# Two layer normalisations moved from VectorE to ScalarE in a three-stage kernel

## The reference

```
x = _layernorm(x + L0_attn(x))     # a state-space layer, 64 heads   -> x1
x = _layernorm(x + L0_ffn(x))      # gated, 704 wide, integer weights -> x2
x = _layernorm(x + L1_attn(x))     # running sums, gated 1024 wide    -> x3
x = _layernorm(x + L1_ffn(x))      # 16 experts, 4 a token            -> out

def _layernorm(x, eps=1e-05):
    return (x - mean(x)) / sqrt(var(x) + eps)
```

## Time and profile before

| what | value |
|---|---|
| median of 3 runs | 2046.97 us (2040.39 to 2054.52) |
| span of the profiled execution, first to last instruction | 2052.9 us |
| that execution's own time | not listed apart from the runs; its span is within their range |
| TensorE matmuls busy | 1773.4 us, 86% |
| TensorE weight loads busy | 1227.3 us, 60% |
| VectorE busy | 1322.3 us, 64% |
| ScalarE busy | 730.2 us, 36% |
| GpSimd busy | 857.8 us, 42% |
| mean granted TensorE clock | 0.948 of full speed |

### The profile page before, as it was taken

The page is one execution under the profiler, slowest core; times in us unless marked ns, Lnnn a source line. Parts: engine busy times, 40 slices in busy tenths (PEclk is TensorE's granted clock), DMA queues, the critical chain, the costliest instruction groups (busy, mean ns, idle before and its releaser), DMA issues. The chain is left out here.

```text
span 2052.9 us, 34902 instructions
## 1 busy us (share of the span) xinstructions
PE 1773.4 (86%) x8724; PEld 1227.3 (60%) x8725; DVE 1322.3 (64%) x2876; ACT 730.2 (36%) x1384; POOL 857.8 (42%) x856
## 2 busy tenths in 40 slices
PE   3589999989999999999998998873899999999980
PEld 2257667667576576676765765652455566666650
DVE  4678878878787888787788787622344444444435
ACT  3244344344343443443444434221222233233223
POOL 2033243333432432433324323223466676666654
PEclk8799999999999999999999999986899999999995
DMA  5423132231231321322313313283999999999997
GB/s 204 141 93 108 28 113 71 69 107 55 82 105 33 111 81 53 107 62 82 107 37 97 103 31 103 71 252 97 195 174 164 171 181 175 173 178 177 176 144 250
DMA packets 385800, 244.37 MB, mean 119 GB/s; under 512 B 269072, under 2 KB 364624, under 8 KB 385360
## 3 DMA queue, kind: packets, MB, share of 16 engines
q1 hardware_dynamic: 319952, 171.79, 32.7%
q0 software_dynamic: 40704, 67.40, 17.7%
q10 hardware_dynamic: 25088, 4.50, 1.2%
HBM read 119.23 MB, written 67.73 MB: 91 GB/s over the span
## 5 line engine op out<-in xcount | busy, mean ns | idle before, releaser
L1675 PE MATMUL pu<-w_all,xh 128*128 x1728 | 363.2, 357 | 53.8 <-DMA xh<-xin 39.0
L1675 PEld LDWEIGHTS pu<-w_all,xh 128*128 128x128 bf16 x1728 | 169.2, 99 | 205.4 <-issue 84.3
L1808 POOL DMA_INDIRECT sums_dram<-yo,meta_in x144 | 229.0, 1591 | 145.5 <-DVE yo L1775 72.6
L1761 DVE TENSOR_TENSOR hid<-pu,gate 128x448 f32<-128x448 f32 x144 | 90.0, 625 | 259.3 <-PE pu L1675 147.6
L836 PE MATMUL pb<-x1T,w_sw 128*128 128x256 f32 x1024 | 231.2, 384 | 0.7 <-ACT x1T L954 0.7
L836 PEld LDWEIGHTS pb<-x1T,w_sw 128*128 128x128 f32 x1024 | 194.1, 192 | 46.2 <-issue 15.5
L1690 PE MATMUL py<-w_all,hh 112*128 x1728 | 212.5, 273 | 1.4 <-DMA hh<-hs 1.4
L1690 PEld LDWEIGHTS py<-w_all,hh 112*128 112x128 bf16 x1728 | 168.7, 98 | 45.1 <-issue 2.1
L1795 POOL DMA_INDIRECT xin<-x_dram,meta_in x144 | 143.1, 993 | 63.0 <-issue 45.9
L650 PE MATMUL pa<-w_in,xT 128*128 128x512 f32 (+1 forms) x384 | 155.0, 549 | 9.1 <-DMA bc_bias<-in_bc_bias 8.4
L1325 DVE SCALAR_TENSOR_TENSOR y<-v,small,y 128x512 f32<-128x512 f32 x224 | 157.8, 746 | 1.2
(11 more groups left out here) (244 smaller groups left out, 3176.4 us busy)
## 6 DMA issues: line engine op xcount, KB each, us to landing
w_stage<-in_w_ug SPq DMA_DIRECT2D x64, 224.0 KB
split_ug<-w_parts SPq DMA_DIRECT2D x64, 224.0 KB
w_all<-split_ug SPq DMA_DIRECT2D x16, 896.0 KB, 9.4
xg_dram<-xg SPq DMA_DIRECT2D x16, 512.0 KB, 3.6
rows<-sums_dram SPq DMA_DIRECT2D x32, 256.0 KB, 5.6
w_stage<-in_w_dn SPq DMA_DIRECT2D x32, 224.0 KB
split_dn<-w_parts SPq DMA_DIRECT2D x32, 224.0 KB
w_all<-split_dn SPq DMA_DIRECT2D x16, 448.0 KB, 10.6
```

The lines of the kernel that those rows point to most:

```text
L1675: last = mm(pu[:, 2 * b + w, 0:EH], xh[:, m % XS, DC * xp + c, :], w_ug[:, bass.ds(e, 1), wp, c, w * EH:(w + 1) * EH], start=n == 0, stop= ...
L1761: vec.tensor_tensor(hid[:, :], pu[:, 2 * (m % 2), 0:EH], gate[:, :], ALU.mult).then_inc(hid_ready.sem, 1)
L1808: nc.gpsimd.indirect_dma_start(out=sums_dram[m % 2], out_offset=bass.IndirectOffsetOnAxis(ap=meta[:, m, 0:1], axis=0), in_=yo[:, m % XS, : ...
```

## The change

x1 and x3 are written by ScalarE, as Identity with scale d and bias offset; VectorE writes only offset1 and offset3, 128 x 2. On ScalarE x1's piece is `A6L-`, between A2 and C7, and x3's piece B6L is the last of the round. Waits that guarded x1 and x3 against overwriting move with them, and VectorE waits before it overwrites r1 and r2 until ScalarE has read them. To make room for two new semaphores, some that were used once in the setup are joined: the setup and the preparation of the feed-forward weights count on one, the clearing of the sums and the padding on another.

```diff
-    "ACT": ("A2 C7 WH.0 A2S F3 B1T C7L C8 A2L B1.0 WH.1 A3 ...
-           "G4+ B5T B5.0 B5.1 B5.2 B5.3 WH.5 B5.4 B5.5 B5.6 B5.7 G3+ A5 A5L"),
+    "ACT": ("A2 A6L- C7 WH.0 A2S F3 B1T C7L C8 A2L B1.0 WH.1 A3 ...
+           "G4+ B5T B5.0 B5.1 B5.2 B5.3 WH.5 B5.4 B5.5 B5.6 B5.7 G3+ A5 A5L B6L"),
...
+        offset1 = sb("offset1", [P, NT, 1])
+        offset3 = sb("offset3", [P, NT, 1])
...
-        dequantised = sig("dequantised", 6)
-        setup_done = sig("setup_done", 1)
+        weights_made = sig("weights_made", 1 + 6)
...
-        sums_cleared = sig("sums_cleared", 16 * 2)
-        padding_stored = sig("padding_stored", 16 * (NE + 1))
+        padding_stored = sig("padding_stored", 16 * (2 + NE + 1))
...
+        offset1_ready, offset3_ready = sig("offset1_ready", 1), sig("offset3_ready", 1)
...
         # ScalarE
+            def normalise(s, src, mv, offset, offset_ready, to, done):
+                act.wait_ge(offset_ready.sem, offset_ready.at(s))
+                for t in range(NT):
+                    act_f(to[:, t, :], src[:, t, :], ACT.Identity, scale=mv[:, t, 1:2], bias=offset[:, t, :]
+                          ).then_inc(done.sem, 1)
+
+            def a6_late(s):
+                if later(s):
+                    act.wait_ge(x2_ready.sem, x2_ready.before(s))
+                normalise(s, r1, mv1, offset1, offset1_ready, x1, x1_ready)
+
+            def b6_late(s):
+                if later(s):
+                    act.wait_ge(x3_stored.sem, x3_stored.before(s))
+                normalise(s, r2, mv2, offset3, offset3_ready, x3, x3_ready)
...
         # VectorE
             def a6(s):
+                if later(s):
+                    dve.wait_ge(x1_ready.sem, x1_ready.before(s))
...
             def a6_late(s):
-                if later(s):
-                    dve.wait_ge(x2_ready.sem, x2_ready.before(s))
-                normalise(s, r1, mv1, norm1, x1, x1_ready)
+                offsets(s, mv1, norm1, offset1, offset1_ready)
...
-            def normalise(s, src, mv, norm, to, done):
+            def offsets(s, mv, norm, offset, done):
                 dve.wait_ge(norm[1].sem, norm[1].at(s))
-                for t in range(NT):
-                    vec.tensor_scalar(to[:, t, :], src[:, t, :], mv[:, t, 0:1], mv[:, t, 1:2], ALU.subtract, ALU.mult
-                                      ).then_inc(done.sem, 1)
+                vec.scalar_tensor_tensor(offset[:, :, :], mv[:, :, 0:1], -1.0, mv[:, :, 1:2], ALU.mult, ALU.mult
+                                         ).then_inc(done.sem, 1)
...
             def b2(s):
                 cb_.start(s)
+                if later(s):
+                    dve.wait_ge(x3_ready.sem, x3_ready.before(s))
...
             def b6_late(s):
-                if later(s):
-                    dve.wait_ge(x3_stored.sem, x3_stored.before(s))
-                normalise(s, r2, mv2, norm3, x3, x3_ready)
+                offsets(s, mv2, norm3, offset3, offset3_ready)
```

More of the change, by code:

```diff
@@ L561, in load_rest @@
                 for sums in sums_dram:
-                    sp.dma_start(sums[nseq * T:nseq * T + P, :], nothing[:, 0:D]).then_inc(sums_cleared.sem, 16)
+                    sp.dma_start(sums[nseq * T:nseq * T + P, :], nothing[:, 0:D]).then_inc(padding_stored.sem, 16)
                 sp.wait_ge(padding_in.sem, padding_in.at(0))
@@ L639, in _ @@
                 sp.wait_ge(piece_stored[n].sem, piece_stored[n].at(NE - 1))
-            sp.wait_ge(sums_cleared.sem, sums_cleared.at(0))
+            sp.wait_ge(padding_stored.sem, padding_stored.at(0))
             sp.wait_ge(x3_stored.sem, x3_stored.at(nseq - 1))
@@ L765, in b1 @@
                     if isinstance(s, int) and s == 0:
-                        pe.wait_ge(dequantised.sem, dequantised.at(0))
+                        pe.wait_ge(weights_made.sem, weights_made.at(0))
                         pe.wait_ge(weights_loaded.sem, weights_loaded.at(0))
@@ L1019, in _ @@
                 "WH": high, "G1": g1, "G2": g2, "G3": g3, "G4": g4, "F3": f3, "A2": a2, "A2S": a2_sin, "A2L": a2_late, "A3": a3,
-                "A3L": a3_late, "A5": a5, "A5L": a5_late, "B1T": b1_first, "B1": b1, "B3T": b3_first, "B3": b3, "B3L": b3_late,
+                "A3L": a3_late, "A5": a5, "A5L": a5_late, "A6L": a6_late, "B6L": b6_late, "B1T": b1_first, "B1": b1, "B3T": b3_first, "B3": b3, "B3L": b3_late,
                 "B5T": b5_first, "B5": b5, "C7": c7, "C7L": c7_late, "C8": c8})
@@ L1166, in _ @@
                 last = vec.tensor_scalar(tok[:, t:t + 1], small[:, SM_P:SM_P + 1], float(t * P), None, ALU.add)
-            last.then_inc(setup_done.sem, 1)
-            dve.wait_ge(setup_done.sem, setup_done.at(0))
+            last.then_inc(weights_made.sem, 1)
+            dve.wait_ge(weights_made.sem, weights_made.at(0, 1))
             def b_and_c():
@@ L1351, in a6_late @@
                         vec.tensor_scalar(w[:, :, :], w[:, :, :].bitcast(I32), -128.0, None, ALU.add
-                                          ).then_inc(dequantised.sem, 1)
+                                          ).then_inc(weights_made.sem, 1)
                     vec.tensor_scalar(w_down[:, 0:FJ - 1, :], w_down[:, 0:FJ - 1, :].bitcast(I32), -128.0, None, ALU.add
-                                      ).then_inc(dequantised.sem, 1)
+                                      ).then_inc(weights_made.sem, 1)
                     r = FH - (FJ - 1) * P
                     vec.tensor_scalar(w_down[0:r, FJ - 1, :], w_down[0:r, FJ - 1, :].bitcast(I32), -128.0, None, ALU.add
-                                      ).then_inc(dequantised.sem, 1)
-                    dve.wait_ge(dequantised.sem, dequantised.at(0, 4))
+                                      ).then_inc(weights_made.sem, 1)
+                    dve.wait_ge(weights_made.sem, weights_made.at(0, 5))
                     vec.tensor_tensor(w_down[:, 0:FJ - 1, :], w_down[:, 0:FJ - 1, :], spread(s_down[:, :], 1, FJ - 1),
-                                      ALU.mult).then_inc(dequantised.sem, 1)
+                                      ALU.mult).then_inc(weights_made.sem, 1)
                     vec.tensor_tensor(w_down[0:r, FJ - 1, :], w_down[0:r, FJ - 1, :], s_down[0:r, :],
-                                      ALU.mult).then_inc(dequantised.sem, 1)
+                                      ALU.mult).then_inc(weights_made.sem, 1)
             def statistics(chain, src, stats, mv, norm):
```

## The result

The changed kernel takes 2142.59 us (median of four runs, 2141.64 to 2150.09) where the kernel before takes 2050.74 (four runs, 2040.39 to 2057.40): 1.046 times as long, interval 1.043 to 1.049. It is slower by 92 us; forecast were 80 from a base 4 us lower. The profiled execution is the longest of the four, 2150.09 us, its span 2148.3.

A forecast was written before the change was run, and what follows sets the result against it. TensorE, working through its written order with its waits, was taken as the bound. Delay 2.6 plus clock 3.0 us over 14 rounds, plus 3 for round 16, less 1 for round 1: +80 on 2046.97, 2127 us; range 2090 to 2155.

The forecast's parts named there:

- The step that decides: At the seam between rounds, x3T's copy queues behind x1 on ScalarE; router 4.54 us late, TensorE stands 4.2 us.
- x3 on ScalarE: At the seam, the scale-and-offset pair takes 1.09 us on ScalarE and delays TensorE's transposes of x3; 0.1 us lost.
- The give-back: Later in the same round, B1T's wait of 0.49 us goes and 1.45 us at ez is cover; 2.6 us remain.
- The clock: After TensorE's stall, router and F3 run partly at 1.2 GHz: 3.0 us a round, added in full, bounds 0 to 4.5.
- the first rival: The clock stays up, or falls in half the rounds, after the stall: 2085 to 2106 us, chance 0.22.
- The sum of the rounds: Rounds 2 to 15 lose 5.6 us each, round 16 some 3, round 1 gains 1: +80 us.
- Table loads: On ScalarE, none taken for the Identity pairs; otherwise 18 to 35 us more.
- VectorE: Loses the x1 and x3 pairs, gains two offsets: 2.86 us a round saved, none of it on the path.
- The faster rival: VectorE and GpSimd's shared port limits the seam, so freeing x1 wins 7 to 28 us: 2019 to 2040, chance 0.03.

The follow-up runs named there:

- the clock kept: The changed kernel, with TensorE doing F3's eight matmuls an extra time ahead of the router from round 2 on, result overwritten; 2107.73 us, ratio 1.026.
- the last experiment: The kernel before, nothing moved to ScalarE, with VectorE's g, which sets off GpSimd's xg product, issued behind x1; 2057.87 us, ratio 1.002.

## Why the prediction was right

**The step that decides** held as written: x3T behind two Identity instructions, and behind x1's offset. TensorE's wait was to be 4.2 us and is 4.28 in the middle rounds. Each half by itself shows that x1 is the whole of it, and x1 behind the sine that its place in ScalarE's order is nearly four fifths. The reason given was too narrow: with x3T copied first the kernel stays 3.7% slower, and TensorE waits 3.07 us for zs, which stands behind the same offset.

**x3 on ScalarE.** From the end of A6 to the end of A2 it is 1.83 us (790.56 to 792.39) against 1.70 before: 0.13, forecast 0.1. By itself x3 costs a little more, 0.5 us from A6 to the router, but half of that comes back by A2L and the time stays the same (1.001). Rows of the combine block gave the pair's 1.09 us to the digit.

**The give-back** of 0.49 and 1.45 us was to leave 2.6 a round. From F3's end to sg it is now 5.7 us (803.87 to 809.59) against 7.6: 1.9 come back, as summed. All parts without the clock: 0.13, 4.44 from A2's end to the router (4.28 against an overlap of 0.16 before), less 1.9, or 2.7 in this trace.

**The clock** was the riskiest term, 3.0 a round out of bounds of 0 to 4.5. It fell in all 14 rounds. F3 takes 5.48 to 6.66 us there, 6.05 in the mean, 2.37 more than before; the router 1.84 in the mean, 0.80 more. Together 3.2, so the price was right. That it "adds in full" was not: with the clock kept, router and F3 take 3.1 us less than in the kernel after, but A2L to w_down takes 1.3 more, so that the round is only 2.3 shorter, and the delay by itself costs 3.6 a round instead of 2.6. The two errors nearly cancel in the sum, which was luck. It also made the first rival too cheap: with the clock up it was to lose 38 us, and the kernel with the clock kept loses 53 (2107.73 against 2054.82). The Trainium skill, page "Perfetto Trace Analysis", section "Matmul Optimizations", says that TensorE scales its power with utilisation and that matmuls should run back to back; filling the hole with matmuls of no use, and getting 1.026 instead of 1.046, agrees.

**The sum of the rounds.** From one router to the next, rounds 2 to 15, it is 87.19 us in the mean against 81.27: 5.9 a round where 5.6 was said. The terms that were mis-sized lie at the two ends. Round 1 was to gain 1 us. Its F3 does start 0.8 us earlier (99.11 against 99.87), but A2L there waits 3.44 us for zs and the projection behind x2n takes 5.40 instead of 3.70, and A6 at its end starts 1.8 us later (177.84 against 176.00). Round 16 was to cost 3; its router waits 4.88 us, and from A6 to the end of the layers 4.6 us are lost. And round 15 has a wait that stands in no term:

```profile
1338.94 2.07 PE L775 MATMUL pb<-x1T,w_gate 128*128 128x256 f32 x4 [3.35 <-DVE hT L1399]
1340.80 1.91 PE L775 MATMUL pb<-x1T,w_up 128*128 128x256 f32 x4
1342.51 1.91 PE L775 MATMUL pb<-x1T,w_gate 128*128 128x256 f32 x4
...
1345.35 1.03 PE L775 MATMUL pb<-x1T,w_gate 128*128 128x256 f32 x4
```

What holds hT up the trace doesn't show; the trace of x1 alone has the same wait at the same place (3.43 us at 1354.84). The clock falls in it too (0.50 from 1339 to 1344), and two of the groups behind it take 1.91 us instead of 1.03. Wait and clock together are 5.8 us more than before. So over the profiled execution it is 1.8 for round 1, 14 rounds of 6.0, 5.8 in round 15 and 4.6 for round 16, or 96 us; its span is 95.4 us longer. The other three runs are 7 to 8 us shorter than this one; whether they have that wait is not recorded. Forecast were 14 of 5.6, 3 for round 16 and 1 less in round 1, or 80.

**Table loads** are none ahead of an Identity: Exp's load stands behind the pair, at 790.44. The Trainium skill, page "ScalarE: Activation LUTs", section "Table sets: the hidden batching unit", has identity in every set; the trace agrees.

**VectorE** saves 3.4 us a sequence (53.8 us over 16) where 2.86 was said. Summed by instruction over the whole execution, the pairs of x1 and x3 less the offsets save 43.0 us, 2.7 a sequence, and ez 18.1, which the sum for VectorE left out; u and one weight preparation (w_up) take 4.2 more. Some of these records overlap, so they don't add up to the busy time to the digit. None of it moves the end. The faster rival, the shared port, was in part tested by the last experiment: x1 was freed of the collision, ez was not, and nothing was won. In the kernel after both are free, and the 1.9 us that come back are what that rival promised; they stand behind a larger loss. The Trainium skill, page "SBUF — State Buffer", section "SBUF: two separate sides", describes one pair of ports that VectorE, for some of its instructions, and GpSimd hold as an exclusive lock for a whole instruction. The trace agrees: x1 takes 2.38 or 0.73 us, bct 2.24 or 0.41, bcr 1.95 or 0.29, as the product meets them. In both experiments that spared x1 the wait it was passed on to the next instruction.

## What to carry to other kernels

An engine that is mostly idle may still be the wrong place for work: ask in what order its queue stands, when the new piece's input is there, and which pieces behind it feed the bound engine. Here 1.1 us of work on an engine busy a third of the time cost 5.9 us a round, because its wait for the offset stood in front of two pieces that TensorE needs, x3T and zs. Price a stall of TensorE with the clock that it loses, but check whether that time and the delay add: here 3.2 us of slower matmuls made 2.3 us of the round. And look for a second piece behind the same wait before moving only the first.

## What was not expected of the hardware

Waits of nearly the same length did not cost the same. With F3 ahead of the router, 14 waits of 2.94 us each brought a slow A2L (13 times 3.35 us or more, once 2.44, against 1.83 at the upper level). With x3T copied first, ten waits of 3.07 to 3.13 us at the same place did so six times; four times the clock stayed at the upper level. In the first kernel the router and B1T stood directly ahead of the wait, in the second F3 and B1T; why the ten split was not settled. It decides much: in the second kernel the rounds with a slow A2L take 85.7 to 89.1 us, and the four of the ten that kept the clock 82.4 to 84.8.
